# Two gathered columns of 31 on TensorE instead of three, from an unsplit fp32 table

## The reference

```python
xw = (x @ W).reshape(N, H, CPH)
a_s = jnp.einsum('nhc,hc->nh', xw, att_src)
a_d = jnp.einsum('nhc,hc->nh', xw, att_dst)
e = jax.nn.leaky_relu(a_s[src] + a_d[dst], NEG)
m = jax.ops.segment_max(e, dst, num_segments=N)
p = jnp.exp(e - m[dst])
s = jax.ops.segment_sum(p, dst, num_segments=N)
alpha = p / s[dst]
out = jax.ops.segment_sum(xw[src] * alpha[:, :, None], dst, num_segments=N)
```

## Time and profile before

| what | us |
|---|---|
| device time, median of 3 executions | 3143.54 (3141.79 to 3145.52) |
| profiled execution: span from first to last instruction | 3949.4 |
| GpSimd busy in the span | 1927.4 |
| VectorE busy | 2043.1 |
| TensorE busy (matmul) | 1918.5 |
| ScalarE busy | 1578.9 |

### The profile page before, as it was taken

How to read it: one execution, slowest core, us unless ns; L and a number is a source line. 1 busy time by engine, 2 the same in 40 slices (tenths; PEclk the granted TensorE clock), 3 DMA queues, 4 the chain that set the end, 5 groups by cost and what they waited for, 6 DMA issues and landing times.

```text
span 3949.4 us, 38354 instructions
## 1 busy us (share of the span) xinstructions
PE 1918.5 (49%) x10116; PEld 1741.9 (44%) x10117; DVE 2043.1 (52%) x4266; ACT 1578.9 (40%) x2552; POOL 1927.4 (49%) x1920
## 2 busy tenths in 40 slices
PE   4500000134435354453544454545213489999998
PEld 2400000123425344353544453435213389999998
DVE  5465676625527355363554563545687544444443
ACT  4322223315536355453555554445323323333332
POOL 4467657645554555535555555465466612222222
PEclk8755555556767676676677776766655599999999
DMA  8244449313332333323333333233365622222222
GB/s 299 76 117 135 144 161 155 120 42 94 94 94 86 94 93 92 94 80 96 94 96 92 94 92 93 59 99 93 119 220 179 230 42 37 36 36 37 36 36 32
DMA packets 212942, 396.68 MB, mean 100 GB/s; under 512 B 76396, under 2 KB 164785, under 8 KB 206305
## 3 DMA queue, kind: packets, MB, share of 16 engines
q1 hardware_dynamic: 136049, 245.72, 18.4%
q0 software_dynamic: 75664, 149.21, 16.8%
q10 hardware_dynamic: 1120, 0.52, 0.0%
HBM read 203.53 MB, written 191.78 MB: 100 GB/s over the span
## 4 chain that ended last, share of the span: by engine, by line
PE 34%; issue 25%; DVE 16%; DVEq 10%; another core or an unknown queue 8%; ACT 4%; SPq 1%; POOL 1%; DMA 1%; POOLq 0%; ACTq 0%
PE ps L1299 13%; PE ps L1390 9%; PE ps L1396 9%; DVEq L1703 5%; DVE AR L1708 4%; PE ps L1270 1%; ACT onehot L1155 1%; ACT AR L1084 1%; DVEq L1709 1%; DVE AR L1773 1%; POOL AR L882 1%; DVE group_stats L1945 1%; ACT onehot L1159 1%; PE ps L1381 1%
## 5 line engine op out<-in xcount | busy, mean ns | idle before, releaser
L882 POOL DMA_INDIRECT AR<-tables,idx x1443 | 1377.0, 954 | 1095.5 <-DMA state<-AR 620.8
L1299 PE MATMUL ps<-table_parts,onehot 128*128 128x408 f32 (+1 forms) x4080 | 953.7, 388 | 1218.1 <-issue 752.5
L1299 PEld LDWEIGHTS ps<-table_parts,onehot 128*128 128x128 f32 x4080 | 861.9, 221 | 1309.9 <-issue 949.7
L1771 DVE TENSOR_SCALAR AR<-ps,tile_pick 128x136 f32<-128x136 f32 x120 | 35.4, 351 | 991.2 <-PE ps L1299 555.4
L1084 ACT COPY AR<-AR 128x1984 f32<-128x1984 f32 (+3 forms) x110 | 392.0, 3564 | 355.1 <-DVE AR L1708 195.6
L956 POOL DMA_INDIRECT out<-AR,idb x105 | 183.5, 1748 | 597.6 <-issue 560.1
L1708 DVE TENSOR_TENSOR_SCAN AR<-ps,AR 128x512 f32<-128x512 f32 x404 | 454.2, 1197 | 0.0
L1390 PEld LDWEIGHTS ps<-AR 128*128 128x128 f32 x3360 | 393.9, 193 | 6.6 <-DVE AR L2164 1.3
L1390 PE MATMUL ps<-AR 128*128 128x128 f32 x3360 | 394.5, 276 | 0.9 <-DVE AR L2164 0.9
L1701 DVE TENSOR_TENSOR AR<-AR,ps 128x3968 f32<-128x3968 f32 (+1 forms) x51 | 356.7, 6994 | 20.7 <-ACT AR L1103 13.4
L1101 ACT ACTIVATE ps<-AR 128x248 f32<-128x248 f32 (+1 forms) x51 | 19.2, 376 | 702.4 <-DVE AR L1688 411.4
(11 more groups left out here) (345 smaller groups left out, 2352.4 us busy)
## 6 DMA issues: line engine op xcount, KB each, us to landing
state<-AR SPq DMA_DIRECT2D x50, 2232.0 KB
AR<-tables,idx POOLq DMA_INDIRECT x1492
AR<-in_L_ffn_W SPq DMA_DIRECT2D x16, 1024.0 KB
AR<-placed SPq DMA_DIRECT2D x105, 130.0 KB, 2.0
adstart<-room SPq DMA_DIRECT2D x26, 496.0 KB
AR<-adstart SPq DMA_DIRECT2D x50, 248.0 KB
tables<-AR SPq DMA_DIRECT2D x49, 136.0 KB
room<-tables SPq DMA_DIRECT2D x14, 476.0 KB
```

Source lines behind the costliest of these rows:

```text
L882: pool.indirect_dma_start(out=G[s][:, j, 0:ROWT], out_offset=None, in_=table_rows, in_offset=bass.IndirectOffsetOnAxis(ap=idx[:, s, j:j + ...
L1299: return T.matmul(bank[:, 0:z], mark, table_parts[:, k, v * w:v * w + z], start=(a == 0 and k == 0), stop=(a == LEV - 1 and k == PARTS - 1))
```

## The change

TensorE fetches two columns of each batch from 10 to 49 instead of three, so GpSimd gathers 29 instead of 28. The table in SBUF is the fp32 table as it is, without parts. Each one-hot matrix is multiplied once, in fp32: 17 products a column, 34 a batch instead of 102. The split on VectorE goes away. The table is loaded once, at batch 7 instead of 5, straight to its place, where rows of `X` lay that are stored by then. The one-hot matrices are 256 wide instead of 384.

```diff
@@ -86,17 +86,12 @@
 PEEL = 8
 ZROW = 2
 ZFIRST = 14
-PEC = 3
-PARTS = 2
+PEC = 2
 PE0, PE1 = 10, NB - 1
-TABLE_AT = 5
-SPLIT_AT = 8
 NPC = PEC * (PE1 - PE0)
 LEV = 17
 TPL = 3
 MIDDLE = float(LEV * P // 2)
-UPPER_BITS = -(1 << 12)
-SPLITS = (((0, 13), (13, 12)), ((25, 12), (37, 12)))
 LEVEL_ORDER = (0, LEV - 1, *range(1, LEV - 1))
 STRETCHES = ((0, 5), (5, 9), (9, 13), (13, 17))
 FIX_B = 7
@@ -159,13 +154,12 @@
         X = AR[:, XO:XO + NT * D].rearrange("p (t d) -> p t d", d=D)
         FB = XO + NT * D
 
-        rounded = mybir.dt.float32r
-        part_size = NT * ROWT
-        table_parts = nc.alloc_sbuf_tensor_at("table_parts", [P, PARTS, part_size], rounded, offset=arena_at + 4 * XO, align_bytes=4)
-        onehot = nc.alloc_sbuf_tensor_at("onehot", [P, LEV, PEC * P], rounded, offset=room_at, align_bytes=4)
-        at = FB + PARTS * part_size - NT * D
+        table_size = NT * ROWT
+        table_tiles = AR[:, XO:XO + table_size]
+        onehot = room[:, 0:LEV * PEC * P].rearrange("p (v e) -> p v e", v=LEV)
+        at = XO + table_size
         column_codes = [a.bitcast(code_type) for a in (AR[:, at:at + PEC * P // 2], room[:, CODES_AT:CODES_AT + PEC * P // 2])]
-        assert at + PEC * P // 2 <= FB + 1152 and LEV * PEC * P <= CODES_AT and CODES_AT + PEC * P // 2 <= ROOM and LEV * TPL >= NT
+        assert at + PEC * P // 2 <= FB and LEV * PEC * P <= CODES_AT and CODES_AT + PEC * P // 2 <= ROOM and LEV * TPL >= NT
         zero = room[:, 0:1024]
         ident = sb("ident", [P, P])
         ones = sb("ones", [P, P])
@@ -463,7 +456,7 @@
         Z, W, R, M8, N8, E8, RM, WP = [a.rearrange("p (h l) -> p h l", l=L) for a in (Z2, W2, R2, M2, N2, E2, RM2, WP2)]
         AI = [a.rearrange("p (h l) -> p h l", l=L) for a in AI2]
         same = cut(5820, C)
-        column_banks = (ps[1], ps[5], ps[6])
+        column_banks = (ps[5], ps[6])
 
         VIEW = {}
         for w, heads in ((L, HD), (WA, HD), (WA, 2 * HD)):
@@ -646,8 +637,15 @@
                 def fetch_codes(b):
                     if b == PE0:
                         sp.wait_ge(lists_stored, 32)
+                        sp.wait_ge(adstart_cleared, 16 * (ZT // ZJ))
+                        sp.wait_ge(zeros_then_pads_stored, 16)
+                        sp.wait_ge(adst_stored, 16)
+                        sp.wait_ge(biased_stored, 16 * NG)
+                        for q in range(RB):
+                            sp.wait_ge(row_stored[q], 16 * (-(-(NT - q) // RB)))
+                        sp.wait_ge(degrees_moved_then_table_loaded, 32)
                         sp.wait_ge(x_rows_stored, 16 * NG)
-                        sp.wait_ge(biased_stored, 16 * NG)
+                        sp.dma_start(table_tiles.rearrange("p (t r) -> p t r", r=ROWT), tab[0].rearrange("(t p) r -> p t r", p=P)).then_inc(degrees_moved_then_table_loaded, 16)
                     n = PEC * (b - PE0) * P
                     sp.dma_start(column_codes[b % 2], flat_codes[n:n + PEC * P].partition_broadcast(P)).then_inc(codes_loaded[b % 2], 16)
 
@@ -692,15 +690,6 @@
                         sp.wait_ge(biased_ready, 2 * (g + 1))
                         sp.dma_start(hbd[g], norm_again.rearrange("p t d -> p (t d)")).then_inc(biased_stored, 16)
                         sp.dma_start(xkept[g], X[:, g * GRP:(g + 1) * GRP, :].rearrange("p t d -> p (t d)")).then_inc(x_rows_stored, 16)
-                    if b == TABLE_AT:
-                        sp.wait_ge(x_rows_stored, 16 * TABLE_AT)
-                        sp.wait_ge(adstart_cleared, 16 * (ZT // ZJ))
-                        sp.wait_ge(zeros_then_pads_stored, 16)
-                        sp.wait_ge(adst_stored, 16)
-                        for q in range(RB):
-                            sp.wait_ge(row_stored[q], 16 * (-(-(NT - q) // RB)))
-                        sp.wait_ge(degrees_moved_then_table_loaded, 32)
-                        sp.dma_start(staging.rearrange("p (t r) -> p t r", r=ROWT), tab[0].rearrange("(t p) r -> p t r", p=P)).then_inc(degrees_moved_then_table_loaded, 16)
                     if b == FIX + 1:
                         sp.wait_ge(links_then_codes_ready, 3)
                         sp.dma_start(codes.rearrange("c p -> p c"), code_out).then_inc(lists_stored, 16)
@@ -1146,7 +1135,6 @@
 
                 n, (first, end) = b - PE0, STRETCHES[i]
                 if i == 0:
-                    act.wait_ge(parts_ready, len(SPLITS))
                     act.wait_ge(codes_loaded[b % 2], 16 * (n // 2 + 1))
                 if n >= 1:
                     act.wait_ge(levels_used, len(STRETCHES) * (n - 1) + i + 1)
@@ -1291,12 +1279,12 @@
                         shift_counts(n)
             project(NT - 1)
 
-            def product(bank, mark, a, k):
+            def product(bank, mark, a):
 
                 v = LEVEL_ORDER[a]
                 w = TPL * ROWT
-                z = min(w, NT * ROWT - v * w)
-                return T.matmul(bank[:, 0:z], mark, table_parts[:, k, v * w:v * w + z], start=(a == 0 and k == 0), stop=(a == LEV - 1 and k == PARTS - 1))
+                z = min(w, table_size - v * w)
+                return T.matmul(bank[:, 0:z], mark, table_tiles[:, v * w:v * w + z], start=(a == 0), stop=(a == LEV - 1))
 
             def columns(b, i):
 
@@ -1306,8 +1294,7 @@
                 pe.wait_ge(marked_by_act, 2 * (len(STRETCHES) * n + i + 1))
                 for a in range(first, end):
                     for c in range(PEC):
-                        for k in range(PARTS):
-                            mm = product(column_banks[c], onehot[:, a, c * P:(c + 1) * P], a, k)
+                        mm = product(column_banks[c], onehot[:, a, c * P:(c + 1) * P], a)
                 mm.then_inc(levels_used, 1)
 
             pe.wait_ge(edge_lists_used, 1)
@@ -1334,7 +1321,7 @@
 
             for n in range(2):
                 chain(n)
-            pe.wait_ge(parts_ready, len(SPLITS))
+            pe.wait_ge(degrees_moved_then_table_loaded, 48)
             for b in range(PE0, PE1):
                 for i in range(len(STRETCHES)):
                     columns(b, i)
@@ -1775,25 +1762,7 @@
                         last.then_inc(columns_taken, 1)
                     dd()
 
-            def split_table(k):
-
-                if k == 0:
-                    dve.wait_ge(degrees_moved_then_table_loaded, 48)
-                    dve.wait_ge(x_rows_stored, 16 * NG)
-                    dve.wait_ge(biased_stored, 16 * NG)
-                for first, n in SPLITS[k]:
-                    a, z = first * ROWT, (first + n) * ROWT
-                    upper = room[:, part_size:part_size + n * ROWT]
-                    V.tensor_scalar(upper.bitcast(I32), staging[:, a:z].bitcast(I32), UPPER_BITS, None, ALU.bitwise_and)
-                    dd()
-                    V.tensor_copy(table_parts[:, 0, a:z], upper)
-                    last = V.tensor_tensor(table_parts[:, 1, a:z], staging[:, a:z], upper, ALU.subtract)
-                    dd()
-                last.then_inc(parts_ready, 1)
-
             def whole_batch(b, w=L, next_w=L):
-                if SPLIT_AT <= b < SPLIT_AT + len(SPLITS):
-                    split_table(b - SPLIT_AT)
                 if by_pe(b):
                     take_columns(b)
                 marks(NA + b, cols(b), same[:, b * J:b * J + cols(b)], VIEW[w, HD], VIEW[next_w, HD] if b + 1 < NB else None)
```

More of the change, by code:

```diff
@@ L296, in build @@
         columns_taken = sem("columns_taken")
-        parts_ready = sem("parts_ready")
         rows_copied = sem("rows_copied")
@@ L478, in build @@
         degree_rows = share_of.rearrange("p a b c t h -> p (a b c t h)")[0:NT, 0:P]
-        staging = room[:, 0:part_size]
         def repeats(w):
```

## The result

The changed kernel takes 3188.11 us (median of 4 executions, 3183.65 to 3191.24), the kernel before 3144.25 us. The ratio is 1.0142, with a 95% interval of 1.0128 to 1.0157: 44 us slower. Forecast were 3181 us, slower, and a range of 3160 to 3215.

A forecast was written before the change was run, and what follows sets the result against it. GpSimd's gathers were taken to bound the 40 batches. One more gather a batch +46.0, the split -6.6 and -1.5, and 0 for the rest gave +37.9 us: from 3143.5 to 3181 us, range 3160 to 3215.

The forecast's parts named there:

- The bound: Batches 10 to 49: GpSimd's gathers bound a timed execution by 5.7 to 9 us a batch; other engines wait.
- ScalarE's and VectorE's smaller work: One-hot work and picks in the 40 batches: both engines wait for GpSimd, so their savings are worth 0.
- One more gather a batch, +46.0: GpSimd, batches 10 to 49: 40 added gathers at 1.15 us cost +46.0 us, bounds +38 to +50.
- if the rest takes as long as in the trace: Condition for time outside the gathers, 1412.4 us, under which a timed gather's pitch is at most 1.20 us.
- A cost of being profiled: TensorE's slow stretches beside gathers: profiling delays, about 20 us for each of 40 batches, explain the missing 805.9 us.
- TensorE hidden: TensorE's loop in the 40 batches becomes 29.8 us against GpSimd's 33.4, hidden with 3.6 us of cover a batch.
- The first rival: TensorE becomes the bound in the 40 batches, 3880 us at half clock throughout; chance 0.07 for anything over 3215.
- The split, -8.1: Twelve VectorE instructions removed at batches 8 and 9: -6.6 us for long gathers, -1.5 us for a scatter's wait.
- The load of the table, 0: Load ahead of batch 10's indices and batch 7's store: covered by gathers, value 0; +15 us without cover.
- the added gather is hidden: GpSimd's waits in timed executions absorb the longer gathers; only the split's gain remains, 3136 to 3145 us; chance 0.07.
- the kernel gets faster: ScalarE and VectorE bound the 40 batches if the pitch is under 1.014 us; 3061 us, chance 0.04.

The follow-up runs named there:

- second profile: The kernel before, unchanged, profiled again: one execution of 3145.26 us, span 3143.5 us, against a span of 3949.4 us in the profile shown before.
- first experiment: The kernel before, profiled again with no edit: one execution of 3145.26 us, span 3143.5 us.

## Why the prediction was right

**The bound.** Shown. With one and two columns in fp32 and three and four in fp32r, the stage is GpSimd's gathers and their pauses and nothing else: 37.45, 36.21, 35.04 and 33.80 us a batch. ScalarE's and VectorE's smaller work was worth nothing, as said: ScalarE's busy time in the stage fell from 992 to 842 us and moved nothing.

**One more gather a batch, +46.0.** The traces have +46.7, but my price of a gather was wrong. I took 1.15 us, and argued that it could be at most 1.20. It is 1401.7 / 1120 = 1.252 us before and 1448.5 / 1160 = 1.249 after. The step that failed is "if the rest takes as long as in the trace". The first gather of batch 0 starts at 236.9 us in the second profile and not at 285, and what follows the last gather takes 1079 us and not 1159. The drawn-out execution was longer at its ends too. With the ends of the second profile the same sum allows a gather (3143.5 - 236.9 - 1079) / 1443 = 1.27 us. One more gather of 1.25 us in 40 batches would be 50; each of the 1160 gathers became 0.003 us shorter, which gives 3 us back and was not foreseen. So the term came out near by luck, with a wrong factor, inside its bounds of 38 to 50.

**"A cost of being profiled".** Wrong. It belonged to one execution (first experiment), and three columns in fp32, with as many TensorE instructions, don't have it: that it grows with their number, as I wrote, is wrong. What saved the argument was that it read durations only in the undisturbed stretches: 1.252 us from gather to gather there is what the second profile has throughout the stage.

**TensorE hidden.** Right, and with more cover than thought. From the experts' products I had 0.356 us for an entry of 408 columns, 23.3 us a batch at full clock. Three columns in fp32 show 33.84 / 51 x 34 = 22.6 us to 23.5. With the 3 us of picks, the loop of the changed kernel is about 26 us at full clock and 28.6 with the 25.6 us that were measured, half clock included. Its cover below 36.2 us is then 8 to 10 us, not 3.6. Of the 4 to 6 us by which 3.6 was too low, 2.8 came from my price of a gather. The first rival (TensorE the bound) needs a third column.

**The split, -8.1.** The part of -6.6 for long gathers was right and a little low: the second profile has 7.1 us beside the split, and the changed kernel has none of it. The part of -1.5 was wrong: the wait of 12.02 us for VectorE isn't there in either kernel (0.30 us ahead of L897 and of L886), so it is 0. Batch 10 starts 9.6 us earlier than before, and 1.7 of the 2.5 us that the split doesn't explain are other long gathers, which add 8.5 us instead of 10.2. Such gathers add 7.0 to 11.0 us in all versions, with and without the split, so I take these 1.7 us for luck and not for an effect of the change.

**The sum.** Forecast +37.9. The two profiled executions have -9.6 ahead of the stage, +46.7 in it and +1.3 behind it, +38.4 in the spans. The medians have +44. The forecast is 6 us below them, and no trace of mine shows where these 6 us are.

**The load of the table, 0.** Right, with a surprise. SyncE's next issue, right behind it, took 10.52 us, so batch 7's store was issued at 602.62 us instead of about 592:

```profile
590.66 0.37 SPq L648 DMA_DIRECT2D AR<-tables  x1
591.08 10.52 SPq L650 DMA_DIRECT2D AR<-codes  x1
...
602.62 0.43 SPq L659 DMA_DIRECT2D state<-AR  x1
```

Batch 10's gathers started at 637.56 us without a wait, so this was covered.

**The other rivals.** That the added gather is hidden needs waits on GpSimd in the stage, and there are none. That the kernel gets faster needs less than 1.014 us from gather to gather, and it is 1.25.

## What to carry to other kernels

Compare the span of a profile with the timed executions before any duration is used, and when it is a quarter longer, take a second profile: idle times and waits of the first one described a kernel that doesn't run. Where one engine issues back to back for a whole stage, a change costs or saves the instructions that it adds to or takes from that engine. Work on the other engines costs nothing until its cover is used up. How much cover is left is found by giving the hidden engine more until it shows (three columns in fp32), and that can point to a better version (four columns in fp32r, 3094 us).

## What the runs showed of the hardware that was not expected

- Right behind the DMA that loads the table (3332 KB in rows of 544 bytes), the next issue on the same queue took 10.52 us, and 10.39 to 11.13 in the four other profiles with this load order, instead of 0.32. In the kernel before, the next issue stands 25 us behind the load (480.16 and 505.91 us) and took 0.32.
- An indirect DMA of 128 rows was issued every 1.25 us in the stage in all kernels bound by it, whatever the other engines did (1.248 to 1.252). It took up to 2.55 us instead of 0.95 beside the split's three kinds of VectorE instructions (bitwise and, copy, subtraction) of 1632 numbers a partition. In the changed kernel a gather issued 0.84 us into a VectorE addition with both operands in SBUF took 2.00 us and ended 0.8 us behind it, while one beside the addition just ahead, with an operand in PSUM (`ps`), kept 0.94:

```profile
347.53 2.02 DVE L1875 TENSOR_TENSOR room<-room,ps 128x1792 f32<-128x1792 f32 x1 [5.65 <-ACT room L1120]
347.81 0.94 POOL L871 DMA_INDIRECT AR<-tables,idx  x1 [0.30 <-issue]
...
349.47 2.02 DVE L1876 TENSOR_TENSOR AR<-AR,bet 128x1792 f32<-128x1792 f32 x1
350.31 2.00 POOL L871 DMA_INDIRECT AR<-tables,idx  x1 [0.30 <-issue]
```

- The granted clock in the stage rose with the density of TensorE's work: 0.70 with 17 fp32 products a batch, 0.87 with 34, 0.97 with 51. In fp32r it was 0.72 with two columns, 0.81 with three, 0.90 with four.
- One execution of the kernel before was 806 us longer, with TensorE's instructions 1.4 us apart beside the gathers; nine other profiles, of this kernel and its variants, don't show it.
